# Second attention: score slots of one PSUM bank in a ring of three, and one reduction for two banks of maxima

## The reference, cut to what matters

```python
ct_q = x @ Wd_q_w + Wd_q_b
query = heads(ct_q @ Wu_q_w + Wu_q_b) + heads(_rope(ct_q @ Wq_r_w + Wq_r_b, cos, sin))
ct_kv = x @ Wd_kv_w + Wd_kv_b
key = heads(ct_kv @ Wu_k_w + Wu_k_b) + heads(_rope(x @ Wk_r_w + Wk_r_b, cos, sin))
value = heads(ct_kv @ Wu_v_w + Wu_v_b)
attn = softmax(einsum('bhqd,bhkd->bhqk', query, key) / scale)
return einsum('bhqk,bhkd->bhqd', attn, value) @ Wo_w + Wo_b
```

## Time and profile before

| | us |
|---|---|
| median of 3 runs | 2366.5 (2366.3 to 2368.9) |
| profiled execution, own time | 2373.8 |
| its span | 2371.8 |
| second attention, maxima to last score | 1407 to 2164 |
| TensorE busy | 1896.3 (80%) |
| VectorE busy | 1509.1 (64%) |
| ScalarE busy | 1120.8 (47%) |
| GpSimd busy | 621.4 (26%) |

### The profile page before, as it was taken

How to read it: one execution, slowest core, us unless ns; L and a number is a source line. 1 busy time by engine, 2 the same in 40 slices (tenths; PEclk the granted TensorE clock), 3 DMA queues, 4 the chain that set the end, 5 groups by cost and what they waited for, 6 DMA issues and landing times. The chain is left out here.

```text
span 2371.8 us, 31808 instructions
## 1 busy us (share of the span) xinstructions
PE 1896.3 (80%) x11577; PEld 675.9 (28%) x11577; DVE 1509.1 (64%) x3101; ACT 1120.8 (47%) x1345; POOL 621.4 (26%) x778
## 2 busy tenths in 40 slices
PE   4508479999999999999569737888888888887879
PEld 2203113333333333333323211211221221122547
DVE  2775556666566656652235557898789889983353
ACT  2321204444444444445142214787777778875422
POOL 0000225554455454433000020420430340110042
PEclk8757659999999999999679867999999999999789
DMA  2100000000000000000110012111110110100414
GB/s 64 39 0 0 1 1 2 20 11 11 11 12 20 11 11 12 11 14 18 26 30 0 1 53 85 38 38 40 45 38 25 49 48 25 46 13 10 139 33 126
DMA packets 57255, 69.83 MB, mean 29 GB/s; under 512 B 23481, under 2 KB 39929, under 8 KB 56973
## 3 DMA queue, kind: packets, MB, share of 16 engines
q1 hardware_dynamic: 55637, 64.59, 8.8%
q0 software_dynamic: 1280, 2.62, 0.4%
q10 hardware_dynamic: 183, 0.59, 0.1%
HBM read 50.11 MB, written 17.01 MB: 28 GB/s over the span
## 5 line engine op out<-in xcount | busy, mean ns | idle before, releaser
L1431 DVE TENSOR_REDUCE h_m_half<-h_ps_max 128x1 f32<-128x512 f32 x1024 | 636.8, 683 | 104.1 <-PE h_ps_max L1178 101.3
L1325 ACT ACTIVATE h_P<-h_ps_st 128x1024 f32<-128x1024 f32 x512 | 495.4, 1021 | 99.9 <-PE h_ps_st L1194 98.3
L803 ACT ACTIVATE l_P<-l_ps_st 128x1024 f32<-128x1024 f32 (+3 forms) x384 | 306.6, 809 | 338.8 <-PE l_ps_st L710 337.3
L710 PE MATMUL l_ps_st<-l_Q,l_K 64*128 64x512 f32 (+3 forms) x1536 | 329.7, 510 | 0.0
L887 DVE CUSTOM_DVE_ANT_0 l_masked<-l_ps_t,l_mask 128x384 bf16<-128x384 f32 (+3 forms) x512 | 230.3, 487 | 111.5 <-PE l_ps_t L668 111.0
L1178 PE MATMUL h_ps_max<-h_K,h_Q 48*128 48x512 bf16 x1024 | 205.6, 398 | 113.6 <-DVE h_m_half L1431 82.9
L1204 PE MATMUL h_ps_o<-h_P,h_V 128*9 128x512 f32 x2048 | 269.3, 598 | 0.7 <-ACT h_P L1325 0.5
L890 DVE TENSOR_REDUCE l_m_half<-l_ps_t 128x1 f32<-128x512 f32 x256 | 164.9, 686 | 105.8 <-PE l_ps_t L668 103.9
L856 POOL TENSOR_SCALAR_AFFINE_SELECT l_P<-l_P 128x256 f32<-128x256 f32 x256 | 102.4, 407 | 416.9 <-ACT l_P L803 416.7
L1194 PE MATMUL h_ps_st<-h_Q,h_K 51*128 51x512 bf16 x1024 | 170.1, 382 | 32.7 <-ACT h_a L1284 6.1
L668 PE MATMUL l_ps_t<-l_Kh,l_Qh 64*128 64x512 bf16 (+3 forms) x768 | 133.2, 342 | 57.7 <-DVE l_m_half L887 43.0
(11 more groups left out here) (309 smaller groups left out, 2359.3 us busy)
## 6 DMA issues: line engine op xcount, KB each, us to landing
l_inv<-inverse_sums SPq DMA_DIRECT2D x64, 128.0 KB
h_inv<-inverse_sums SPq DMA_DIRECT2D x60, 128.0 KB, 2.8
y_rows<-zero SPq DMA_DIRECT2D x8, 512.0 KB, 4.9
c_W<-in_W SPq DMA_DIRECT2D x16, 256.0 KB, 5.4
c_back<-y_rows SPq DMA_DIRECT2D x16, 256.0 KB, 4.9
k_parts<-h_parts SPq DMA_DIRECT2D x4, 768.0 KB, 4.3
q_parts<-h_parts SPq DMA_DIRECT2D x4, 768.0 KB, 4.1
h_Q<-q_parts SPq DMA_DIRECT2D x31, 96.0 KB
```

The source lines that it names most:

```text
L710: last = pe.matmul(ps_st[x % 2][:, a, 0:w], K[n // NG % 2][rows, kt * 128:(kt + 1) * 128], Q[n % NQ][rows, p, q0:q0 + w], start=True, stop ...
L803: act.activation(P[e % PR][:, :, 0:w], ps_st[item(n, i, p) % 2][:, :, 0:w], ACT.Exp, scale=0.125).then_inc(consumed, 1)
L1325: act.activation(P[e % PR][:, :, :], ps_st[x % 2][:, :, :], ACT.Exp, scale=1.0 / 12.0).then_inc(consumed, 1)
L1431: dve.tensor_reduce(m_half[:, half, 2 * p + a, qt:qt + 1], ps_max[:, t % NB, :], AX.X, ALU.max, negate=True)\
```

## The change

The constants become NB = 2 and NST = 3. `ps_st` is now three slots of one bank, `ps_max` two buffers of two banks; the sum stays eight banks. `order` names each score product (its p and its half a) and each half of a projection by itself; `free_slot` waits for item x-3. Each score product and each exponential of 512 columns has its own count; a projection is made and evicted in two halves. `maxima` gives one count for its two products and waits for the reduction two pairs back; one reduction reads both banks and writes two values. In an iteration the order on TensorE is scores p = 0, maxima, scores p = 1, maxima, values; before it was scores, scores, maxima, values, maxima.

```diff
-    NB, PR, NBUF, NOB, NLOAD, MIX = 3, 4, 4, 7, 12, 16
+    NB, NST, PR, NBUF, NOB, NLOAD, MIX = 2, 3, 4, 4, 7, 12, 16
...
+    def halves(key):
+        return [(key, c) for c in range(2)] if key[0] != "out" else [(key, 0)]
...
-            order += [("s", n, i, p) for p in range(2)]
+            order += [("s", n, i, p, a) for p in range(2) for a in range(2)]
             if (n, i) in AT:
-                order.append(AT[n, i])
+                order += halves(AT[n, i])
...
-        ps_st = [ctx.enter_context(nc.psum_tensor(f"h_ps_st{i}", [128, 2, CH], F32)) for i in range(2)]
-        ps_max = ctx.enter_context(nc.psum_tensor("h_ps_max", [128, NB, CH], F32))
+        ps_st = [ctx.enter_context(nc.psum_tensor(f"h_ps_st{i}", [128, CH], F32)) for i in range(NST)]
+        ps_max = [ctx.enter_context(nc.psum_tensor(f"h_ps_max{i}", [128, 2, CH], F32)) for i in range(NB)]
...
             def free_slot(x):
-                if x >= 2:
-                    pe.wait_ge(consumed, x - 1)
-                return ps_st[x % 2]
+                if x >= NST:
+                    pe.wait_ge(consumed, x - NST + 1)
+                return ps_st[x % NST]
...
-                    for c in range(2):
-                        cols = slice(c * CH, (c + 1) * CH)
-                        src = ct[...] or S.hT[...]
-                        last = pe.matmul(to[:, cols], w, src, start=True, stop=True)
+                    src = ct[...] or S.hT[...]
+                    last = pe.matmul(to[:, :], w, src, start=True, stop=True)
...
-                t = 2 * (n * NPAIR + u)
-                if t + 2 > NB:
-                    pe.wait_ge(reduced, t + 2 - NB)
+                t = n * NPAIR + u
+                if t >= NB:
+                    pe.wait_ge(reduced, t + 1 - NB)
                 for a in range(2):
                     rows = slice(64 * a, 64 * a + D6)
-                    pe.matmul(ps_max[:, (t + a) % NB, :], Q[...], K[...], start=True, stop=True).then_inc(max_ready, 1)
+                    last = pe.matmul(ps_max[t % NB][:, a, :], Q[...], K[...], start=True, stop=True)
+                last.then_inc(max_ready, 1)
...
             def scores(n, i, p):
-                to = free_slot(item["s", n, i, p])
                 for a in range(2):
-                    last = pe.matmul(to[:, a, :], K[...], Q[...], start=True, stop=True)
-                last.then_inc(st_ready, 1)
+                    to = free_slot(item["s", n, i, p, a])
+                    pe.matmul(to[:, :], K[...], Q[...], start=True, stop=True).then_inc(st_ready, 1)
...
                     for p in range(2):
+                        s = 2 * i + p + HALF + LEAD
                         scores(n, i, p)
-                    for s in (2 * i + HALF + LEAD, 2 * i + 1 + HALF + LEAD):
                         maxima(n + s // NPAIR, s % NPAIR)
-                        if s % 2 == 0 and n + i:
-                            values(n if i else n - 1, (i - 1) % NI)
+                    if n + i:
+                        values(n if i else n - 1, (i - 1) % NI)
...
-                        act.activation(P[e % PR][:, :, :], ps_st[x % 2][:, :, :], ACT.Exp, scale=1.0 / 12.0).then_inc(consumed, 1)
+                        for a in range(2):
+                            x = item["s", n, i, p, a]
+                            act.wait_ge(st_ready, sum(k[0] != "turn" for k in order[:x]) + 1)
+                            act.activation(P[e % PR][:, a, :], ps_st[x % NST][:, :], ACT.Exp, scale=1.0 / 12.0).then_inc(consumed, 1)
...
-                    for a in range(2):
-                        t = 2 * (n * NPAIR + u) + a
-                        dve.wait_ge(max_ready, t + 1)
-                        dve.tensor_reduce(m_half[:, half, 2 * p + a, qt:qt + 1], ps_max[:, t % NB, :], AX.X, ALU.max, negate=True)\
-                           .then_inc(reduced, 1)
+                    t = n * NPAIR + u
+                    dve.wait_ge(max_ready, t + 1)
+                    dve.tensor_reduce(m_half[:, half, 2 * p:2 * p + 2, qt:qt + 1], ps_max[t % NB][:, :, :], AX.X, ALU.max, negate=True)\
+                       .then_inc(reduced, 1)
```

More of the change, by code:

```diff
@@ L983, in head_attention @@
             AT[(b + 1) * NG + 2, 4 + 6 * c] = ("out", b, c)
-    order = [(x, 0) for x in PROJECT] + [("turn", 0)]
+    def halves(key):
+        return [(key, c) for c in range(2)] if key[0] != "out" else [(key, 0)]
+    order = [y for x in PROJECT for y in halves((x, 0))] + [("turn", 0)]
     for n in range(NGR):
@@ L1045, in mix @@
             at = base + (1 - u) * (MIX // 2)
-            eng.wait_ge(consumed, item[("qu", "ku")[u], b] + 1)
+            eng.wait_ge(consumed, item[(("qu", "ku")[u], b), 1] + 1)
             eng.tensor_tensor(a[:, :], a[:, :], cos[:, :], ALU.mult).then_inc(done, 1)
@@ L1136, in free_slot, with half_product @@
             def free_slot(x):
-                if x >= 2:
-                    pe.wait_ge(consumed, x - 1)
-                return ps_st[x % 2]
+                if x >= NST:
+                    pe.wait_ge(consumed, x - NST + 1)
+                return ps_st[x % NST]
             def product(key):
-                kind, b, x = key[0], key[1], item[key]
-                to = free_slot(x)[:, :, :].rearrange("p a c -> p (a c)")
+                for half in halves(key):
+                    half_product(key[0], key[1], half)
+            def half_product(kind, b, half):
+                c = half[1]
+                cols = slice(c * CH, (c + 1) * CH)
+                to = free_slot(item[half])
                 if kind == "v":
[L1145 to L1148, removed]
+                    pe.wait_ge(consumed, item[("ct", b), 1] + 1)
+                    for t in range(KT // 2):
+                        keys = slice((c * KT // 2 + t) * 128, (c * KT // 2 + t + 1) * 128)
+                        last = pe.matmul(to[:, t * 128:(t + 1) * 128], ct[64:128, keys], Wkv[64:128, 1, :], start=True, stop=True)
                 elif kind == "out":
                     pe.wait_ge(normed, 2 * NG * (b + 1))
-                    c = key[2]
+                    c = half[0][2]
                     for g in range(NG):
-                        last = pe.matmul(to[:, 0:CH], Wo[:, g, :], o[(b * NG + g) % NOB][:, c * CH:(c + 1) * CH],
+                        last = pe.matmul(to[:, :], Wo[:, g, :], o[(b * NG + g) % NOB][:, c * CH:(c + 1) * CH],
                                          start=(g == 0), stop=(g == NG - 1))
@@ L1158, in product @@
                     if kind[0] == "q" or kind == "ku":
-                        pe.wait_ge(consumed, item["ct", b] + 1)
-                    for c in range(2):
-                        cols = slice(c * CH, (c + 1) * CH)
-                        src = ct[0:64, cols] if kind[0] == "q" else ct[64:128, cols] if kind == "ku" else S.hT[:, batch(b, c)]
-                        last = pe.matmul(to[:, cols], w, src, start=True, stop=True)
+                        pe.wait_ge(consumed, item[("ct", b), c] + 1)
+                    src = ct[0:64, cols] if kind[0] == "q" else ct[64:128, cols] if kind == "ku" else S.hT[:, batch(b, c)]
+                    last = pe.matmul(to[:, :], w, src, start=True, stop=True)
                 last.then_inc(st_ready, 1)
@@ L1172, in maxima @@
                 qt, p, lo = u // 4, (u // 2) % 2, (u % 2) * CH
-                t = 2 * (n * NPAIR + u)
-                if t + 2 > NB:
-                    pe.wait_ge(reduced, t + 2 - NB)
+                t = n * NPAIR + u
+                if t >= NB:
+                    pe.wait_ge(reduced, t + 1 - NB)
                 for a in range(2):
                     rows = slice(64 * a, 64 * a + D6)
-                    pe.matmul(ps_max[:, (t + a) % NB, :], Q[n % NBUF][rows, p, qt * 128:(qt + 1) * 128],
-                              K[n % NBUF][rows, p, lo:lo + CH], start=True, stop=True).then_inc(max_ready, 1)
+                    last = pe.matmul(ps_max[t % NB][:, a, :], Q[n % NBUF][rows, p, qt * 128:(qt + 1) * 128],
+                                     K[n % NBUF][rows, p, lo:lo + CH], start=True, stop=True)
+                last.then_inc(max_ready, 1)
             def turn(h):
@@ L1193, in scores @@
                     rows = slice(64 * a, 64 * a + D6 + MP)
-                    last = pe.matmul(to[:, a, :], K[n % NBUF][rows, p, kt * 128:(kt + 1) * 128],
-                                     Q[n % NBUF][rows, p, c * CH:(c + 1) * CH], start=True, stop=True)
-                last.then_inc(st_ready, 1)
+                    to = free_slot(item["s", n, i, p, a])
+                    pe.matmul(to[:, :], K[n % NBUF][rows, p, kt * 128:(kt + 1) * 128],
+                              Q[n % NBUF][rows, p, c * CH:(c + 1) * CH], start=True, stop=True).then_inc(st_ready, 1)
             def values(n, i):
                 kt, b, g = i % KT, n // NG, n % NG
-                pe.wait_ge(consumed, item["s", n, i, 1] + 1)
+                pe.wait_ge(consumed, item["s", n, i, 1, 1] + 1)
                 if kt == 0 and (n or i):
@@ L1210, in spread_last_sums @@
```

(38 more changed lines are left out.)

14 lines of the change are left out of this document (7 added, 7 removed).

## The result

| | us |
|---|---|
| before, median of 4 runs | 2366.4 |
| after, median of 4 runs | 2400.5 (2399.9 to 2402.6) |
| ratio, 95% interval | 1.0145 (1.0127 to 1.0162) |
| forecast, range | 2389.5, 2366 to 2410 |

A forecast was written before the change was run, and what follows sets the result against it. It took a 2.47 us loop of VectorE's reductions and TensorE as the bound, replaced by a 2.60 us score-exponential loop. 23+0.5+5.0-6.1 = +22.5, taken as 23, on 2366.5 gave 2389.5 us; range 2366 to 2410.

The forecast's parts named there:

- The old loop through the first reduction, M0, V and M1: Kernel before: reduction, first maxima pair, value products, second maxima pair in turn set the iteration at 2.47 us.
- One reduction for two: VectorE: one reduction of 1024 replaces two of 512, about 1.14 us per pair instead of 1.20.
- k3 waits for e0 of its own iteration, with V behind it: Three score slots: an iteration's fourth score waits some 0.4 us for its first exponential, the value products queued behind.
- e1 to e3: ScalarE: an iteration's second to fourth exponentials follow at about 0.50 us each and leave ScalarE idle before the next iteration's first.
- The loop forecast: New loop through TensorE and ScalarE, fourth score to the next iteration's fourth score: 2.60 us, +0.13 on 2.47.
- k0's start to e0's start: Term of the new loop, from the start of an iteration's first score to that of its first exponential: 0.43 us.
- Products in halves: In the score loop, projections made and evicted in halves: +2.09 us for each of 24; output products +3.81 each.
- Value-bank evictions and turns: Per group, two value-bank evictions delay the next first exponential by 0.18 us each; two maxima turns add 0.17 each.
- Rival (a): The score slot is released before the exponential's recorded end: loop 2.50 us, 2365 us in all, no change; chance 0.10.
- Rival (b): VectorE's rate decides the score loop: iteration 2.28 us, 2307 us in all, faster; chance 0.06.
- Rival (c): The fourth score alone on the upper rows breaks TensorE's pairing: +0.22 us an iteration, 2443 us; chance 0.07.
- Rival (d): TensorE's new stops cost clock: a tenth of the iterations at 4.0 us, +34, 2423 us; chance 0.08.
- e2: ScalarE: exponential of an iteration's third score, the first of p = 1; about 0.50 us after the one before.

The follow-up runs named there:

- the two reductions: The changed kernel with its merged reduction undone, two reductions of 512 columns per pair of maxima: ratio 1.014 to the kernel before, period 2.65 us.
- The run with four slots: The changed kernel with four single score slots, and maxima, their reductions and TensorE's order as before the change: ratio 0.9948 to the kernel before, period 2.47 us.
- wait_swap: The changed kernel with ScalarE's two waits before an iteration's first exponential in the old order, score first: ratio 1.0095 to the kernel before, period 2.59 us.

## Why the prediction was right, point by point

- The old loop through the first reduction, M0, V and M1 was there and went away: TensorE's wait for the reductions fell out of the list. Right.
- One reduction for two: 1222 ns (1220 expected), two in 2.36, so 1.14 apart. VectorE's work fell by 30.3 us, the 31 that the prediction took from rows and not the 64 beside it. Right, and worth nothing in the loop, as the two reductions showed; ahead of the loop a pair takes 1.13 (1.14 expected).
- k3 waits for e0 of its own iteration, with V behind it: right, and shown from three sides: e0's length moves the period by 0.21, the lengths of e1 to e3 don't, and M1 taken out of the loop takes its 0.22 with it. The run with four slots agrees, but changes the maxima too. The stop before k3 is 0.31, where some 0.4 was expected.
- The period was 2.65, not 2.60. The loop forecast has every other term right within 0.01; the term mis-sized is k0's start to e0's start: 0.43 was read off the kernel before and is 0.48 here. The swap of the waits gives it back (0.42, period 2.59). The change had also exchanged the two waits of ScalarE before an exponential, which the full diff shows, and I gave that no price. 240 iterations times 0.05 are 12 us, which is what the stretch from the first score to group 15 has over its forecast (34.6 against 23). A group is 43.0 instead of 42.3.
- Products in halves: an iteration with one and its successor take 4.56 + 2.85 in the changed kernel (k0 to k0), 2.11 over two plain ones (2.09 expected); with an output product 6.28 + 3.10, against 2.65 + 2.81 without one that is 3.9 (3.81). Right.
- Value-bank evictions and turns: 2.79 and 2.81 against 2.65, 0.14 and 0.16 (0.18 and 0.17). Right.
- Rival (a), an earlier release, is excluded by k3's start 0.66 behind e0's start (0.60 and 0.06). Rival (b), VectorE's rate, by its idle 0.30. Rival (c): k3 and the first product of M1 start together at 1609.98, so the pairing holds across different pairs. Rival (d): the granted clock is 1.00 from 1480 to 2200 us; the cycling of banks with a stop in every iteration did not make it swing, so what the Trainium skill tells (TensorE: Matmul & The Clock Gate, A second HAM failure mode: psum-queue depth-cycling) did not happen here. In one place the prediction read the kernel before too well: from 1690 to 1700 us, where TensorE stopped 1.04 us before the scores behind a projection, its granted clock was 0.83. The changed kernel has no such place in the loop after 1480 us.

## What to carry to other kernels

When slots get finer, ask for each item which earlier item frees its slot: if that is one of the same iteration, and a long operation stands between them in the in-order queue of the producer, the ring is a loop, and where it is the longest one its sum is the period, whatever the engines' busy shares say. Find what stands in that loop without need, and move it into the wait that the loop itself makes. Time saved counts only in an operation that lies in the loop: half of e0 was worth 0.21 an iteration, half of e1, e2 and e3 on the same engine nothing.

## What was not expected of the hardware

ScalarE starts an exponential 0.42 us after its score has started if the wait for that score stands before another wait that is already met, and 0.48 us if it is the last before the operation (0.42 in `wait_swap`, 0.42 to 0.43 in the kernel before; 0.48 in the changed kernel, 0.47 with four slots, 1770.65 to 1771.12). The other wait is for value products that end, as modelled, 0.41 us before e0 starts in the changed kernel (1610.51 and 1.05 long, e0 at 1611.97). What in the engine makes the 0.05 stays open: only the order of the two waits was tried.

TensorE's queue is in order for a product that waits: nothing behind k3 starts before it. The start of running products can differ from their order in the code. In the kernel before, one score product starts at 1501.12 us, ahead of the last two passes of the projection issued before it:

```profile
1500.67 1.02 PE L1163 MATMUL h_ps_st<-h_ct,h_Wu 64*128 64x512 f32 x2
1501.12 0.39 PE L1194 MATMUL h_ps_st<-h_Q,h_K 51*128 51x512 bf16 x1
1501.54 1.02 PE L1163 MATMUL h_ps_st<-h_ct,h_Wu 64*128 64x512 f32 x2
```

The projection uses 64 rows of the array; that the score runs on the other 64 is read from the code, and no run tests it.
